# A two-layer graph kernel: one-hots before the last rows, 108-column slot placement, an earlier scaling, and a final normalization without its mean

## What is computed

```python
def _layernorm(x, axis=-1, eps=1e-05):
    m = jnp.mean(x, axis=axis, keepdims=True)
    v = jnp.var(x, axis=axis, keepdims=True)
    return (x - m) / jnp.sqrt(v + eps)

def _L0_gnn_ref(node_feat, edge_feat, eps, src, dst):
    m = jax.nn.relu(node_feat[src] + edge_feat)
    neigh = jax.ops.segment_sum(m, dst, num_segments=node_feat.shape[0])
    return (1.0 + eps[0]) * node_feat + neigh

def _L1_gnn_ref(node_f, src, dst):
    ones = jnp.ones(src.shape[0], dtype=node_f.dtype)
    out_deg = jnp.clip(jax.ops.segment_sum(ones, src, num_segments=n), 1.0)
    in_deg = jnp.clip(jax.ops.segment_sum(ones, dst, num_segments=n), 1.0)
    x = node_f * jax.lax.rsqrt(out_deg)[:, None]
    agg = jax.ops.segment_sum(x[src], dst, num_segments=n)
    return agg * jax.lax.rsqrt(in_deg)[:, None]

x = _layernorm(x + _L0_gnn_ref(x, edge_attr_32, L0_gnn_eps, src, dst), axis=-1)
x = _layernorm(x + _L1_gnn_ref(x, src, dst), axis=-1)
```

## Time and profile before

| | |
|---|---|
| median of 3 runs | 5188.48 us (5188.18 to 5191.56) |
| profiled execution: its own time | 5192.55 us |
| its span, first to last instruction | 5190.4 us |
| PE busy | 3318.3 us (64%) |
| DVE busy | 3288.3 us (63%) |
| ACT busy | 2750.1 us (53%) |
| POOL busy | 2966.5 us (57%) |

### The profile page before, as it was taken

How to read it: one execution, slowest core, us unless ns; L and a number is a source line. 1 busy time by engine, 2 the same in 40 slices (tenths; PEclk the granted TensorE clock), 3 DMA queues, 4 the chain that set the end, 5 groups by cost and what they waited for, 6 DMA issues and landing times. The chain is left out here.

```text
span 5190.4 us, 62756 instructions
## 1 busy us (share of the span) xinstructions
PE 3318.3 (64%) x21148; PEld 1678.6 (32%) x21148; DVE 3288.3 (63%) x4729; ACT 2750.1 (53%) x2907; POOL 2966.5 (57%) x3134
## 2 busy tenths in 40 slices
PE   4555555555555555555555555555555999999997
PEld 1111111111111111111111111111113888888886
DVE  7766666666666666666666666666666444444445
ACT  4555555555555555555555555555553555555553
POOL 7777777777777777777777777777772000000000
PEclk7666666666666666666666666666666999999998
DMA  3333333333333333333333333333335999999995
GB/s 125 120 119 136 126 119 119 120 126 128 131 123 119 119 119 119 131 131 119 119 120 124 124 136 123 119 119 119 119 128 179 326 325 323 326 324 325 325 325 206
DMA packets 269133, 867.70 MB, mean 167 GB/s; under 512 B 90218, under 2 KB 140218, under 8 KB 252602
## 3 DMA queue, kind: packets, MB, share of 16 engines
q1 hardware_dynamic: 169107, 815.98, 42.3%
q0 software_dynamic: 100000, 51.40, 5.3%
HBM read 486.77 MB, written 380.38 MB: 167 GB/s over the span
## 5 line engine op out<-in xcount | busy, mean ns | idle before, releaser
L166 POOL DMA_INDIRECT rows<-in_x,src_t x3125 | 2964.8, 949 | 959.5 <-issue 946.1
L688 PE MATMUL built<-x_parts,b_hot 100*128 100x490 bf16 x3000 | 1292.6, 534 | 1758.3 <-ACT big L622 1743.2
L622 ACT ACTIVATE big<-built 128x980 bf16<-128x980 f32 x1500 | 1805.0, 1229 | 546.2 <-PE built L688 542.9
L688 PEld LDWEIGHTS built<-x_parts,b_hot 100*128 100x128 bf16 x3000 | 249.9, 111 | 2647.8 <-ACT big L622 2029.4
L1061 PE MATMUL applied<-counts,x_parts 128*96 128x160 bf16 x12250 | 916.1, 233 | 17.5 <-DVE x_parts L873 17.5
L427 DVE TENSOR_TENSOR sum_ps<-sum_ps,rows 128x416 f32<-128x416 f32 x250 | 143.0, 572 | 1229.9 <-DMA rows<-in_x,src_t 1224.7
L668 PE MATMUL agg<-hot,msg 128*128 128x512 bf16 x3125 | 903.2, 440 | 4.9 <-DVE msg L457 4.9
L1061 PEld LDWEIGHTS applied<-counts,x_parts 128*96 128x96 bf16 x12250 | 880.2, 123 | 80.7 <-issue 18.8
L146 DVE TENSOR_TENSOR x_parts<-iota_ps,hk_g 100x3920 bf16<-100x3920 f16 x375 | 819.5, 2185 | 0.0
L1017 ACT ACTIVATE counts<-built 128x980 bf16<-128x980 f32 x496 | 594.3, 1239 | 387.5 <-PE built L1044 387.5
L146 DVE TENSOR_TENSOR hot<-iota_ps,s_hi 128x5252 bf16<-128x5252 f16 x250 | 691.4, 2766 | 0.0
(11 more groups left out here) (135 smaller groups left out, 1445.4 us busy)
## 6 DMA issues: line engine op xcount, KB each, us to landing
stash<-big SPq DMA_DIRECT2D x125, 2940.0 KB
counts<-stash SPq DMA_DIRECT2D x250, 1470.0 KB, 8.7
rows<-in_x,src_t POOLq DMA_INDIRECT x3125
edge_t<-in_edge_attr SPq DMA_DIRECT2D x61, 800.0 KB
big<-in_dst SPq DMA_DIRECT2D x1, 1562.5 KB
big<-in_src SPq DMA_DIRECT2D x1, 1562.5 KB
src_t<-in_src SPq DMA_DIRECT2D x61, 24.8 KB
dst_t<-in_dst SPq DMA_DIRECT2D x61, 24.8 KB
```

The costliest lines, as they stand in the source:

```text
L166: gp.indirect_dma_start(rows_d[:, j, :], None, nodes, bass.IndirectOffsetOnAxis(ap=src_d[:, j:j + 1].bitcast(U32), axis=0),).then_inc(s, 16)
L622: sc.activation(stage[:, slot % 2, q, :, d0:d0 + 2 * SPAN].rearrange("p c (b d) -> p b c d", b=2), built[n % 2][:, :, 0:KEYS].rearrange("p ...
L688: last = te.matmul(built[n % 2][:, b, 0:KEYS], b_hot[:, r, t, :], key_hot[:, r, t, :], start=True, stop=True)
```

## The change

Four edits:

1. In step g = G of layer 0, DVE does `indices()`, the read-out of the sums before, and five of its six blocks of one-hots ahead of `add(0)`; the memset follows `left(0)`. What is left behind the rows is the relay of parts with `lo_hot(0)` in it. The other steps are as they were.
2. `place_hot`, `put` and the window of `acc_1` are WD = 108 columns wide instead of W = 128.
3. The scaling of `x_0`, the square root and the reciprocal of `r_in` move from step k = NC to step k = NC - 1.
4. The finish leaves out the mean: the sum of a scaled aggregate of rows with mean zero and a row with mean zero has mean zero already. `mean` and `centred` are replaced by `summed`; ACT does both squares before both roots.

```diff
+                            if isinstance(g, int) and g == G:
+                                ve.wait_ge(z_part2[1], g - 1)
+                                indices()
+                                sums_out()
+                                ve.wait_ge(z_idx[3], g)
+                                dst_hot(0)
+                                hi_hot(0)
+                                hi_hot(1)
+                                dst_hot(1)
+                                lo_hot(1)
                                 add(0)
                                 left(0)
                                 for k in range(2):
                                     ve.wait_ge(z_stash[k], (NC + 1 - k) // 2 * 16)
                                 ve.memset(x_0[P - 32:P, TAIL:C, :], 0.0).then_inc(z_clear, 1)
                                 last_part(0)
+                                lo_hot(0).then_inc(z_hot, 1)
                                 add(1)
                                 left(1)
                                 last_part(1)
...
-                place_hot = sb("place_hot", [HS[0], 2, W], BF16)
+                place_hot = sb("place_hot", [HS[0], 2, WD], BF16)
...
-                put = small[A1:A1 + D, 2 * D:2 * D + W]
+                put = small[A1:A1 + D, 2 * D:2 * D + WD]
...
-                                window = acc_1[:, bass.ds(first, W)]
+                                window = acc_1[:, bass.ds(first, WD)]
...
-                            if isinstance(k, int) and k == NC:
+                            if isinstance(k, int) and k == NC - 1:
                                 ve.tensor_tensor(x_0[:, :, :], x_0[:, :, :], wide(rstd, 0, C), ALU.mult).then_inc(l_rin, 1)
                                 ve.wait_ge(l_root, 1)
                                 ve.reciprocal(r_in[:, :], r_in[:, :]).then_inc(l_rin, 1)
...
-                            if isinstance(k, int) and k == NC:
+                            if isinstance(k, int) and k == NC - 1:
                                 sc.activation(r_in[:, :], r_in[:, :], ACT.Sqrt).then_inc(l_root, 1)
...
+                        def summed(h):
                             c0, c1 = PART[h]
                             ve.wait_ge(h_used, (CUT, len(FR))[h])
+                            ve.tensor_tensor(y[:, c0:c1, :], y[:, c0:c1, :], x_n[:, c0:c1, :], ALU.add).then_inc(h_summed, 1)
...
                         for k in range(CUT):
                             normed(k)
-                        mean(0)
-                        normed(CUT)
-                        centred(0)
-                        for k in range(CUT + 1, len(FR)):
+                        summed(0)
+                        for k in range(CUT, len(FR)):
                             normed(k)
+                        summed(1)
                         variance(0)
-                        mean(1)
                         result(0)
-                        centred(1)
                         variance(1)
                         result(1)
...
+                        squares(0)
+                        squares(1)
+                        deviation(0)
+                        deviation(1)
```

More of the change, by code:

```diff
@@ L464, in step, with sums_out @@
                                 chunk(0, 0, 0)
-                            if sends(g):
+                            def sums_out():
+                                ve.wait_ge(z_agg, g - 1)
+                                ve.tensor_tensor(degree[:, :], degree[:, :], agg_degree, ALU.add)
+                                ve.tensor_copy(taken[:, :], agg).then_inc(z_taken, 1)
+                            if isinstance(g, int) and g == G:
[8 more added lines that the diff above has]
+                                lo_hot(1)
                                 add(0)
-                            if builds(g):
-                                chunk(g, k, 1)
-                            if sends(g):
                                 left(0)
-                                indices()
-                            if isinstance(g, int) and g == G:
                                 for k in range(2):
@@ L475, in step @@
                                 ve.memset(x_0[P - 32:P, TAIL:C, :], 0.0).then_inc(z_clear, 1)
[L476 to L482, removed]
                                 last_part(0)
-                                ve.wait_ge(z_idx[3], g)
-                                dst_hot(0)
+                                lo_hot(0).then_inc(z_hot, 1)
                                 add(1)
-                                hi_hot(0)
                                 left(1)
[L491 to L494, removed]
                                 last_part(1)
+                            else:
+                                if sends(g):
+                                    add(0)
+                                if builds(g):
+                                    chunk(g, k, 1)
+                                if sends(g):
+                                    left(0)
+                                    indices()
+                                if adds(g):
+                                    sums_out()
+                                if builds(g):
+                                    chunk(g, k, 2)
+                                if sends(g):
+                                    last_part(0)
+                                    ve.wait_ge(z_idx[3], g)
+                                    dst_hot(0)
+                                    add(1)
+                                    hi_hot(0)
+                                    left(1)
+                                    lo_hot(0).then_inc(z_hot, 1)
+                                    hi_hot(1)
+                                    lo_hot(1)
+                                    dst_hot(1)
+                                    last_part(1)
                             if adds(g):
@@ L981, in step @@
                                 for h in range(2):
-                                    ve.tensor_scalar(place_hot[0:HS[h], h, :], iota[0:HS[h], :], place[0:HS[h], h, bass.ds(k - 2, 1)], None, ALU.is_equal)
+                                    ve.tensor_scalar(place_hot[0:HS[h], h, :], iota[0:HS[h], 0:WD], place[0:HS[h], h, bass.ds(k - 2, 1)], None, ALU.is_equal)
                                 ve.wait_ge(l_slot, k - 1)
@@ L1285, in _, with squares, deviation @@
                     def _(sc):
[L1286 to L1287 removed]
+                        def squares(h):
+                            c0, c1 = PART[h]
+                            sc.wait_ge(h_summed, h + 1)
                             sc.activation(sq[:, c0:c1, :], y[:, c0:c1, :], ACT.Square).then_inc(h_squares, 1)
+                        def deviation(h):
+                            c0, c1 = PART[h]
                             sc.wait_ge(h_var, h + 1)
                             sc.activation(rstd[:, c0:c1], var[:, c0:c1], ACT.Sqrt, bias=ln_eps[:, 0:1], scale=1.0 / D).then_inc(h_dev, 1)
+                        squares(0)
+                        squares(1)
+                        deviation(0)
+                        deviation(1)
                     @block.sync
```

16 lines of the change are left out of this document (1 added, 15 removed).

## The result

The changed kernel takes 5166.98 us (median of 6 runs, 5165.13 to 5168.62), the kernel before 5188.26 us (6 runs, 5186.44 to 5191.56): a ratio of 0.9958, 95% interval 0.9948 to 0.9968. That is 21.3 us less; 20.6 were forecast, and 5167.9 us for the time.

The account below looks back on a forecast made before the run. POOL's gathers were taken to bound layer 0, PE's stream layer 1, and neighbours' waits the tails and finish. Gains 4.9 + 5.9 + 2.1 + 7.7 = 20.6 us, off the median 5188.48, gave 5167.9 us; range 5160 to 5180.

Parts of the forecast that it names:

- Part 1: Layer 0's last step: one-hots moved ahead of add(0) let PE's last sum start 4.9 us earlier.
- the late `add(0)`: Layer 0's last step: moved blocks make add(0) start some 1.2 us later than the rows allow.
- Its other bound, the clock: Layer 0's last sum: all 25 at 1.2 GHz gain 3.7 us less, all at 2.4 GHz 1.7 more.
- Part 2: Layer 1's steps: placement in 108 columns saves 0.048 us each for 124 placements, 5.9 us.
- The first rival: Layer 1: narrower puts bring nothing, since a floor, shape switch or transfers set the pace; 5173.8 us, chance 0.20.
- Part 3: End of layer 1: with the scaling one step sooner, the last slots are split 2.1 us earlier.
- Part 4: Finish: leaving out the mean shortens the chain of mostly DVE work by 7.7 us.
- the schedule T + 22.9: Finish: result(1), the last multiplication, ends 22.9 us after the transposes start; before, it was 30.6 us.
- The two stores: End of the finish: the second store follows by 4 instead of 7 us and may touch the first, up to 1 us.
- The sum: Whole kernel: the four gains add, 4.9 + 5.9 + 2.1 + 7.7 = 20.6 us.
- The third rival: Finish: transposes find the clock high and PE's pace halves, some 4.8 us more gain; 5163.1 us, chance 0.06.
- The slower rival: Layer 1: PE's granted clock drops; each us at 1.2 GHz costs 0.5 us, 80 us give 5208; chance 0.03.

Follow-up runs that it names:

- e4_hots_back: Changed kernel with the order of DVE's last step of layer 0 put back as before; 5172.38 us (6 runs).
- e1_wide128: Changed kernel with the placement (place_hot, put and window) put back to 128 columns; 5173.94 us (7 runs).
- e5_scale_back: Changed kernel with the scaling of x_0, the root and the reciprocal put back in step NC; 5171.55 us (one run).
- e6_mean_back: Changed kernel with the finish of before, mean included, put back; 5178.40 us (one run).
- e3_put32: Changed kernel with the placement cut to 32 columns, leaving out edge sums of the columns beyond; 5147.48 us (one run).
- e10_warm_all: Changed kernel with its own waits filled, plus idle PE multiplications ahead of layer 0's last sum and at three more places; 5163.65 us (4 runs).
- e7_warm_finish: Changed kernel with 17 idle PE multiplications around the last placement at the end of layer 1; 5169.27 us (one run).

## Why the prediction was right

Range, sign and size held, and nearly every term by itself.

- **Part 1, 4.9 us.** 4.84 in the first pair, but its closeness is in part luck: the kernel before had its rows early and its clock up early in that profile. It is 5.8 on average over all profiles (5.2 from the start, 0.6 from the clock in the sum), less 0.36 given back in the normalization, which the prediction didn't have; 5.4 by the times of e4_hots_back. `add(0)` started 8.09 us behind group 124's sums (8.1 by the prediction's own schedule) in all seven runs with this order, however late the rows were, while with the old order it followed the rows (6.92, 7.39 and 7.43 us). The prediction charged the late `add(0)` with 1.2 us; with the rows of the other two profiles of the old order it is 0.7. Its other bound, the clock, was real: the same 25 multiplications took 5.4 to 8.2 us over all runs. In the first pair the clock rose 2.8 and 2.9 us after the sum's start, so nothing of it showed.
- **Part 2, 5.9 us.** 6.2 by e1_wide128. The line through 160 and 490 columns held down to 64. The first rival, with 0.20 the heaviest, was wrong: the floor is there, near 25 ns, and far from 45.
- **Part 3, 2.1 us.** 2.5 by e5_scale_back, of which 2.1 are the wait and 0.3 a clock that had fallen in that run. In the two profiles of the kernel before, the same idleness cost the last placements 0.04 us and nothing, so 2.1 to 2.2 is the edit's own worth.
- **Part 4, 7.7 us.** 7.8 by e6_mean_back; the schedule T + 22.9 was T + 22.81. The two stores did not hold each other up: the tail went from 4.22 to 4.24 us.
- **The sum.** 5.8 - 0.4 + 6.2 + 2.5 + 7.8 = 21.9 us by the single edits, 20.4 by the first pair of profiles, 21.3 by the times, 20.6 forecast.
- **The third rival** (fast transposes) would have been wrong even where its condition is met, as far as six transposes at clock 1.00 can show: its price of 4.8 us took the transposes to go with the clock. So the range's lower end, 5160, rested on a mechanism that no run shows.
- **The slower rival.** The clock stayed at 1.00 in layer 1's full stretch, and the step got shorter by the full columns; nothing of it was seen.

## What to carry over

Where one engine's queue bounds a stage, look at what the others do after its last item: that tail is paid once, but in full, and all that doesn't need the last item belongs ahead of it. Price such an edit as a schedule of the timeline from the last fixed event, with the handovers in it, and count from that event when profiles are compared; here the unchanged stage ahead scattered by as much as a single edit is worth. Undoing each edit by itself also finds what it costs elsewhere, here 0.36 us in a stage that it doesn't touch. In a stream of short multiplications that never idles, columns that hold only zeros cost their full time, until a floor that one run with far fewer columns finds.

## What the runs showed of the hardware

- Six bf16 multiplications with weights of 80 by 32 go at their columns' pace from 128 down to 64 columns; at 32 columns they start 25 ns apart (e3_put32), where columns alone would give 13.3 + 3.
- fp32 transposes of 32 by 128 take 0.12 us each at granted clock 0.50, and so do the six that began at 1.00 in e10_warm_all. 98 of them in a row, PE busy for 11.8 us, don't raise the clock (the changed kernel, columns as in the earlier trace rows); in e10_warm_all it fell while they ran.

```profile
5136.00:5147.00 11.00, 11.00 (x94) 11.00 (x94) 5.68 (x7) 1.50 (x1) 0.00 (x0) 0.50 0.01 2
```

- From layer 1 to the finish, the first transpose follows the last work of the last engine by 2.6 us: DVE's add in the kernels before and after, PE's idle work in e7_warm_finish and e10_warm_all.
- Rows gathered by POOL were at hand 2.4 to 3.2 us after the last gather began in the five profiles without idle work on PE in that time in which DVE waited for them, and 4.3 and 4.8 us in the two with it. The cause is open.
- With one-hots ahead of `add(0)`, a DVE instruction 45 us later starts 0.46 us after the ACT instruction it waits for, and 0.10 us after it with the old order, the same in every profile of either kind. The cause is open.
